# Eight normalised tiles on GpSimd and two sums of W moved: the start of a rails stage

## The reference, cut to what matters

```python
xr = x.reshape(b, t, RAILS, RAIL_W)               # x: the layer norm, 64 rails of 16
y = jnp.einsum('btri,hrij->bthrj', xr, rail_maker)
z = jnp.einsum('bthrj,hrkj->bthrk', y, rail_up_proj)
h = jax.nn.gelu(z.reshape(b, t, -1), approximate=False)
out = h @ w_cproj.T                               # 16384 hidden units to 1024
```

## Time and profile before

| what | value |
|---|---|
| median of three runs | 2593.78 us (2592.81 to 2595.72) |
| the profiled execution, first to last instruction | 2589.7 us |
| mean granted TensorE clock, share of full speed | 0.978 |
| PE, DVE, ACT, POOL busy | 2465.5, 1968.1, 1230.4, 143.8 us |
| the rails stage | from about 504 to about 2000 us |

### The profile page before, as it was taken

The page is one execution under the profiler, slowest core; times in us unless marked ns, Lnnn a source line. Parts: engine busy times, 40 slices in busy tenths (PEclk is TensorE's granted clock), DMA queues, the critical chain, the costliest instruction groups (busy, mean ns, idle before and its releaser), DMA issues. The chain is left out here.

```text
span 2589.7 us, 34729 instructions
## 1 busy us (share of the span) xinstructions
PE 2465.5 (95%) x12652; PEld 1666.1 (64%) x12652; DVE 1968.1 (76%) x2504; ACT 1230.4 (48%) x1413; POOL 143.8 (6%) x173
## 2 busy tenths in 40 slices
PE   6999299889999999999999999999999989999998
PEld 4666287756666666666666666666666556568776
DVE  7876799798888897797797788788788756665422
ACT  6322676565555455445545545545544235522111
POOL 1000000010000000000000000000000011000222
PEclk9999699989999999999999999999999999999999
DMA  5211311143232232322421422422331045836993
GB/s 164 63 39 39 67 40 40 67 141 62 73 63 57 75 61 57 88 49 55 95 57 41 96 56 41 96 56 47 88 105 49 1 136 178 264 135 211 353 379 109
DMA packets 145389, 252.12 MB, mean 97 GB/s; under 512 B 67128, under 2 KB 82106, under 8 KB 138838
## 3 DMA queue, kind: packets, MB, share of 16 engines
q1 hardware_dynamic: 135378, 231.40, 31.3%
q0 software_dynamic: 4928, 10.25, 1.6%
q10 hardware_dynamic: 4932, 8.30, 0.9%
HBM read 204.01 MB, written 49.33 MB: 98 GB/s over the span
## 5 line engine op out<-in xcount | busy, mean ns | idle before, releaser
L1761 PE MATMUL wide_ps<-keep_own_room,rails_hid_hi 128*125 128x512 f16 x4200 | 1250.7, 379 | 5.2 <-DVE rails_hid_lo L1478 3.2
L1761 PE MATMUL wide_ps<-keep_own_room,rails_hid_lo 128*125 128x512 f16 x2100 | 796.4, 379 | 0.0
L1761 PEld LDWEIGHTS wide_ps<-keep_own_room,rails_hid_hi 128*125 128x125 f16 x4200 | 564.7, 137 | 312.5 <-issue 6.4
L1761 PEld LDWEIGHTS wide_ps<-keep_own_room,rails_hid_lo 128*125 128x125 f16 x2100 | 286.9, 137 | 167.0 <-issue 0.6
L1253 ACT ACTIVATE rails_hid_hi<-rails_raw_a,keep_scale_hidden 128x1000 f16<-128x1000 f32 x210 | 274.5, 1334 | 209.5 <-DVE rails_raw_a L1497 90.8
L1478 DVE SCALAR_TENSOR_TENSOR rails_hid_lo<-rails_raw_a,keep_scale_hidden,rails_hid_hi 128x1000 f16<-128x1000 f32 x210 | 312.1, 1516 | 41.7 <-ACT rails_hid_hi L1253 41.6
L1243 ACT ACTIVATE rails_raw_a<-wide_ps,keep_scale_gelu 128x1000 f32<-128x1000 f32 (+1 forms) x192 | 181.6, 951 | 323.6 <-PE wide_ps L1746 320.2
L1532 DVE SCALAR_TENSOR_TENSOR keep_X<-wide_ps,rails_out_scale,keep_X 125x1024 f32<-125x1024 f32 x180 | 198.6, 1103 | 132.3 <-PE wide_ps L1761 132.3
L1486 DVE SCALAR_TENSOR_TENSOR keep_own_room<-carried_w_land,rails_w_scale,keep_own_room 128x2048 f16<-128x2048 f32 x105 | 246.0, 2343 | 0.7 <-ACT keep_own_room L1268 0.7
L1268 ACT ACTIVATE keep_own_room<-carried_w_land,rails_w_scale 128x2048 f16<-128x2048 f32 x105 | 208.9, 1990 | 9.8 <-DVE carried_w_land L1516 5.7
L1228 ACT ACTIVATE rails_raw_a<-carried_w_land 128x2048 f32<-128x2048 f32 x64 | 121.7, 1902 | 141.9 <-DMA carried_w_land<-cproj 141.7
(11 more groups left out here) (476 smaller groups left out, 3359.3 us busy)
## 6 DMA issues: line engine op xcount, KB each, us to landing
carried_w_land<-cproj SPq DMA_DIRECT2D x79, 1024.0 KB
ffn_w_up<-split_d SPq DMA_DIRECT2D x9, 2048.0 KB
keep_own_room<-W SPq DMA_DIRECT2D x11, 1024.0 KB, 5.8
ffn_w<-W SPq DMA_DIRECT2D x11, 1024.0 KB
rails_xs<-xt_d SPq DMA_DIRECT2D x124, 78.1 KB
keep_comb_hi<-W SPq DMA_DIRECT2D x8, 1024.0 KB, 7.2
split_d<-graph_high SPq DMA_DIRECT2D x16, 512.0 KB, 6.6
keep_X<-split_d SPq DMA_DIRECT2D x4, 2048.0 KB
```

Source lines behind the costliest of these rows:

```text
L1761: mm = nc.tensor.matmul(ps[0:P, t, :], hid[(q + b) % 2][l][:, k, t * P:(t + 1) * P], w[(q + b) % 2][r][:, k, :], start=(k == 0 and i == 0) ...
```

## The change

GpSimd's list gets the normalising of tiles 2 to 9, with the same two waits that VectorE had (tile t - 3 transposed; the late statistics, now a wait on the semaphore of `late_rstd_of`). The largest value of b11's sums is taken between tiles 8 and 9, those of b12 and b22 after tile 9; before, the order was b12, b11, b22. On VectorE the late statistics follow tile 0's low part, their aggregation tile 1's, the reciprocal tile 2's, and the low parts of tiles 3 to 7 follow one another. On ScalarE the sum of b11 stays behind tile 5's high part and is now the first; those of b12 and b22, which were behind tiles 3 and 7, come after the high part of the last piece of the first hidden block and before `w_hi(0, 1, 0)`. Scale 0 of the first unit waits for one largest value in place of two. The order of the sums in later units is as before.

```diff
@@ gpsimd @@
-                for name in ("b12", "b11", "b22"):
-                    spread_top(name, 0)
+                def normalise(t):
+                    if t >= 3:
+                        pool.wait_ge(xt_turned, t - 2)
+                    if t == HALF_T:
+                        pool.wait_ge(late_rstd, 2)
+                    nc.gpsimd.tensor_scalar(xn[t % 3], X[:, t, :], mean_var[:, t, 0:1], rstd_up[:, t:t + 1],
+                                            ALU.subtract, ALU.mult).then_inc(xn_set, 1)
+
+                def first_top(name, n):
+                    pool.wait_ge(summed, n)
+                    nc.gpsimd.partition_all_reduce(tops[:, TOP[name]:TOP[name] + 1], sums[:, TOP[name]:TOP[name] + 1], 128,
+                                                   bass.bass_isa.ReduceOp.max).then_inc(top_set, 1)
+
+                for t in range(2, TILES - 1):
+                    normalise(t)
+                first_top("b11", 1)
+                normalise(TILES - 1)
+                first_top("b12", 2)
+                first_top("b22", 3)
@@ scalar: w_sum @@
-                    if not isinstance(u, int) or 4 * u + k >= 1:
+                    if not isinstance(u, int) or u >= 1 or name == "b21":
                         act.wait_ge(summed, 4 * u + k)
+                    elif name != "b11":
+                        act.wait_ge(summed, 1 if name == "b12" else 2)
@@ scalar: the prologue @@
-                    if t == 3:
-                        w_sum("b12", 0, "a12", None)
                     if t == 5:
                         w_sum("b11", 0, "a12", None)
-                    if t == 7:
-                        w_sum("b22", 0, "a12", None)
                 w_hi(0, 0, 0)
...
                 a_hi(0, 0, 0, 1)
+                w_sum("b12", 0, "a12", None)
+                w_sum("b22", 0, "a12", None)
                 w_hi(0, 1, 0)
@@ vector @@
-                    dve.wait_ge(top_set, 4 * u + k + 2)
+                    dve.wait_ge(top_set, 1 if k == 0 and isinstance(u, int) and u == 0 else 4 * u + k + 2)
...
                 attention_out()
-                normalise(2)
                 x_lo(0)
-                normalise(3)
+                late_stats()
                 x_lo(1)
-                late_stats()
-                normalise(4)
+                late_layer_of()
                 x_lo(2)
-                late_layer_of()
-                x_lo(3)
                 late_rstd_of()
-                normalise(5)
-                normalise(6)
-                x_lo(4)
-                normalise(7)
-                x_lo(5)
-                normalise(8)
-                x_lo(6)
-                normalise(9)
-                x_lo(7)
+                for t in range(3, 8):
+                    x_lo(t)
                 scale_of(0, 0)
```

More of the change, by code:

```diff
@@ L1404, in late_rstd_of @@
                     dve.wait_ge(late_rstd, 2)
-                def normalise(t):
-                    if t >= 3:
-                        dve.wait_ge(xt_turned, t - 2)
-                    nc.vector.tensor_scalar(xn[t % 3], X[:, t, :], mean_var[:, t, 0:1], rstd_up[:, t:t + 1],
-                                            ALU.subtract, ALU.mult).then_inc(xn_set, 1)
                 def x_lo(t):
```

## The result

| what | before | after |
|---|---|---|
| median of four runs | 2593.44 us (2592.81 to 2595.72) | 2630.14 us (2628.98 to 2631.15) |
| ratio, 95% interval | | 1.0138 [1.0124, 1.0151] |
| profiled execution, first to last instruction | 2589.7 us | 2627.2 us |
| mean granted TensorE clock | 0.978 | 0.969 |
| first product, from tile 0's transpose | 32.79 us | 64.65 us |

The account below looks back on a forecast made before the run. It took the rails stage's prologue (504 to 553 us) as decisive, TensorE being full afterwards, so delays shift everything. 2593.78 us - 0 (prologue) + 5.4 (t3 behind the sums) + 0.8 (clock) = 2600.0 us; range 2595.0 to 2604.2.

Parts of the forecast that it names:

- Tiles 2 to 9 on GpSimd: Prologue up to the first product: eight normalises moved from VectorE to GpSimd, hidden by other waits, 0 us.
- The late statistics: Statistics that tiles 5 to 8 wait for in the prologue: ready at about 515.7 us, against 518.2 before.
- Rival A: GpSimd becomes the prologue's bound, one normalise taking 3.4 us: 5.4 us more than forecast, 2605.4; chance 0.07.
- T: Time of one normalise on GpSimd: taken as 1.0 to 1.3 us, hidden if under 2.7 us.
- The transfers set the loads of x: Prologue: the busy DMA queue, not VectorE, sets when x is loaded (issued 526.71) and hidden matmuls start (530.08).
- Rival B: Prologue shortens if VectorE, not transfers, set the first five tiles' stores: 2.7 us sooner, 2597.3; chance 0.10.
- The sums and t3: Behind the first hidden block, VectorE's t3 waits for ScalarE's two moved sums, delaying everything behind it: +5.4 us.
- the clock: New TensorE gaps behind the first product may lower its clock: 0 to 1.6 us, taken as +0.8.
- The rule on the shared port: VectorE's t3 and b22's all-reduce shut each other out: all-reduce ends some 2.0 us later, sum unchanged.
- The range: Bounds on the whole kernel's time, from above the sums-fit rival to short of Rival A: 2595.0 to 2604.2 us.

Follow-up runs that it names:

- price list: The kernel before, with a chain of 22 GpSimd operations at the rails stage's start, each waiting for the last; only its rows count, no kernel time given.
- experiment 3: After, plus a one-column tensor_scalar on GpSimd in the attention stage, ahead of the rails stage: 2616.58 us, ratio 1.0086.
- experiment 4: After, with b11's largest value taken behind tile 9's normalise, so no all-reduce between normalises: 2625.11 us, ratio 1.0123.
- experiment 6: After, with both the early one-column tensor_scalar and b11's largest value taken behind tile 9's normalise: 2613.43 us, ratio 1.0073.
- experiment 11: Before, with a chain of 18 GpSimd operations, including all-reduce and memset ahead of the first tensor_scalar, iota and affine select; only rows count, no kernel time given.
- experiment 7: Before, with b21's W load issued after the loads of x instead of ahead of them: 2591.68 us in one run.
- experiment 8: Before, with b21's load after the loads of x, b12's sum at tile 2 and late statistics ahead of tile 3's normalise: 2592.64 us, ratio 0.9993.
- experiment 10: Before, with b21's load after x's, square root behind b12's sum, late aggregation, reciprocal and tile 5's normalise moved ahead of tile 4's: 2593.61 us, ratio 0.9996.
- experiment 1: Before, with only the sums of b12 and b22 and the order of largest values changed, normalises left on VectorE: 2599.21 us, ratio 1.0017.
- experiment 2: After, with the sums and the order of the largest values put back, normalises staying on GpSimd: 2624.44 us, ratio 1.0114.
- experiment 5: The price list: before, with a chain of 22 GpSimd operations at the rails stage's start; no kernel time given.
- experiment 9: Before, with only tiles 2 to 4 normalised on GpSimd, plus a one-column tensor_scalar in the attention stage: 2595.57 us, ratio 1.0.

## Why the prediction was wrong, step by step

**The failed step: "Tiles 2 to 9 on GpSimd", costed at nothing.** Two things were wrong in it.

First the duration. I took 1.0 to 1.3 us from the memset and the cast and had 3.4 us as the upper end; a normalise takes 3.78, above that end. The cast that I leaned on writes uint16, not float columns as I had it. The price list shows why the nearest rows misled: memset, cast and copy move data, and the three other rows with arithmetic at 1024 columns lie at 1.89, 2.79 and 3.63. The Trainium skill (GPSIMD Engine Reference, Engine selection) has GpSimd about twice as slow as VectorE for two-input work, and "1-input is roughly line-rate". If that is VectorE's rate, the copy agrees roughly, 1.04 us against 0.80 of VectorE's normalise; the tensor_scalar does not, 3.78 against 0.80, and the measurement decides.

Second, the larger part, a cost that I had no term for: between tensor_scalar and all-reduce GpSimd stands still. In after the steps are 11.5 us ahead of the first normalise, 5.80 ahead of b11's all-reduce and 7.21 ahead of tile 9's normalise. Their rows make up the path to the first product: 11.5 of the first step, 11.4 for three normalises, 3.8 waiting for the statistics, 15.1 for five more, 5.8 and 0.4 for the all-reduce, 7.2 and 3.8 for tile 9, and 5.7 from there to the product, 64.7 together, of which 32.8 were there before. Experiments 3, 4 and 6 take steps away one by one: 11.9, 5.4, and together 16.5 us of the 31.9. The remaining 15.4 are the last step and the normalises (experiment 6); how these two share it no run tells apart. An estimate from its rows: b11's all-reduce starts 8.26 us ahead of the first product in experiments 4 and 6 alike (555.03 to 563.29, 543.87 to 552.13), so its step counts whole, about 6, and the normalises take the other 9, if nothing else would hold the product by then.

Could it have been seen? Rows of before's own trace that I had not read, far behind the prologue, on GpSimd, and two of its queue:

```profile
2093.59 0.24 POOL L1961 IOTA graph_order_i<- 125x100 int32 x1 [76.94 <-issue]
...
2104.49 0.38 POOL L1972 PARTITION_ALL_REDUCE graph_part_tops<-graph_part_sums  x1 [7.66 <-issue]
...
2317.29 0.23 POOL L2508 IOTA ffn_res<- 125x80 int32 x1 [43.53 <-issue]
```

```profile
L1961 POOLq MODIFY_POOL_CONFIG  x2: 11/11/11, 2083.4 to 2083.5; - x2
L2508 POOLq MODIFY_POOL_CONFIG  x2: 11/11/11, 2310.0 to 2310.0; - x2
```

Both iotas are the first in their stage's list, behind all-reduces of the stage before, and wait for no semaphore of their own; they start 10.2 and 7.3 us behind their pairs. The all-reduce starts 7.66 us behind the iota and memset ahead of it (there the sum's wait may lie in the gap as well; experiment 11 gives 5.92 us for iota to all-reduce). So before had the kind of cost and its size, with "issue" as the releaser; that tensor_scalar stands on iota's side was not to be had from it. The Trainium skill (GPSIMD Engine Reference, Instruction dispatch) has a price too: the first call of freshly loaded GpSimd code costs some 6 us that no instruction in a profile shows, counted from MODIFY_POOL_CONFIG. The 5.5 to 6.1 us from pair to all-reduce in the rails stage agree with that figure, if each change of kind counts as a first call; the 7 us back and the 10 to 13 us do not. That code is loaded is that page's word: the runs show the pair at each change, and not what GpSimd does behind it.

**The late statistics: wrong in its consequence.** I put them at 515.7, at the latest 518.2. On GpSimd's side they counted at 530.31 (3.81 us idle for them), because the square root follows tile 4's high part, and tile 4 came late.

**Rival A, GpSimd as the bound: right in kind, wrong in price.** With T = 3.4 and no steps it came to 5.4 us more than the forecast. T was 3.78 and the steps were the larger part.

**The transfers set the loads of x: right for before, not for after.** Experiment 7 moves them by 2.4 us with one load less ahead, and with GpSimd's first step gone they stay within 0.9 us of where they were (experiment 3). In after the tiles came later than the transfers did. Rival B took a gain there to reach the first product whole, 2.7 us; experiment 7 gave 0.8 of 2.4, and experiments 8 and 10, which move other work as well, 0.9 and 1.2.

**The sums and t3: right, with some luck at TensorE.** +5.4 forecast, 5.43 us of idling in after and in experiment 1; at a22's last hidden part experiment 1 is 6.2 us behind before (559.95 - 505.29 = 54.66 relative, for 48.49), as much as the forecast, and the runs give 4.7 with an interval that holds it. The way was another: one wait of 5.23 us, not three, which makes 5.5; then 0.4 where the clock was put at 0.8; and 0.2 that lie ahead of the first product, where the forecast had nothing.

**The rule on the shared port: borne out, at no cost.** In after b22's all-reduce (573.39) was over 0.3 us after t3 had begun (573.43) and took 0.35 us, which tells nothing. In experiment 2 the all-reduce started at 569.05 while t3 ran (568.44, 2.29 us), took 1.92 us and ended 0.24 us after t3, as at 624.38 in before; scale 1 asked for it only at 572.34.

**The range.** It let GpSimd's prices run from 0.87 to 3.4 us for one operation and had no term for what lies between two operations; the price of an operation that the trace does not show was bounded (too low), the price of a new kind of operation on an engine was not.

## What to carry to other kernels

An operation that an engine has not run before in a stage has two prices, its own and that of the change from the operations beside it; on GpSimd look for "issue" idle of 6 to 13 us where iota or arithmetic on tensors meets an all-reduce, and for MODIFY_POOL_CONFIG in its queue, and keep the two kinds apart, or let the change fall where nothing waits. To price an operation that the trace lacks, take rows that compute as much for each element, not rows that move as many. And where one wait is taken away, name the engine that has no gap behind it: three edits that freed the loads of x by 2.3 to 2.6 us gave the product 0.8 to 1.2.

## What the runs showed of the hardware, unexpected

- Of GpSimd's operations tried here, two kinds displace each other: tensor_scalar, tensor_tensor and iota on one side, the partition all-reduce on the other. In the rails stage 5.7 to 6.1 us of idling lie ahead of the all-reduce and 6.9 to 7.4 on the way back, at every change that no wait covers; memset, copy and affine select stood beside the all-reduce for nothing, and the affine select and memset do not undo a change. A pair of MODIFY_POOL_CONFIG instructions in the queue marks each change (experiments 5 and 11).
- A program's first tensor_scalar waited 10.8 to 12.8 us (five kernels). In before an iota that is not the program's first waited as long (10.2 us behind its pair, some 2080 us after the last of its side), and the next one, 222 us after that, 7.3. What the extra 3 to 5 us are stays open.
- Whether a wait for a semaphore hides the change depends on which stands first in the queue. In experiment 9 the wait ended at 518.5, the pair followed at 518.9, and the all-reduce came at 525.02, 6.5 us after the sum. In after the pair stood ahead of the wait (562.8), the sum was done at 571.2, and the all-reduce came at 571.33.
- A tensor_scalar of GpSimd with two column operands took 3.7 ns a column (3.78 us for 1024), VectorE's 0.78.
